# Tile 0's multi-query preparation moved into the last feed-forward block, and mixing weights applied to the queries

## The chip, the cores and the metric

One core of one Trainium2 chip runs the whole kernel in one launch. The metric is device time in microseconds. PE is TensorE, PEld its weight load, DVE is VectorE, ACT is ScalarE, POOL is GpSimd, SP is SyncE, which issues the DMAs.

## The reference

Input x is 16 sequences of 256 tokens with 128 channels, fp32. Four residual layers follow each other, each on a layer-normalised input:

```python
x = x + attn_a(layernorm(x))   # 32 heads of 4, two decaying scans (m = 0, 1), own layer norm
x = x + ffn(layernorm(x))      # sum over 8 experts of (silu(x Wg) * (x Wu)) Wd, FFN 512
x = x + attn_b(layernorm(x))   # 16 query heads of 8, one key and value head, causal softmax
x = x + ffn(layernorm(x))      # the same weights again

# attn_a, per token; phi(u) = elu(u) + 1, beta clipped, mix a softmax over m
S = S * beta[m] + phi(k) v
K = K * beta[m] + phi(k)
num, den = phi(q) . S, phi(q) . K + eps
y = sum over m of num / den * mix[m]
```

## The kernel before

A tile is 512 tokens, that is two sequences; there are 8. The program has three stages, and each engine's order of instructions is written out by hand. Engines meet at counting semaphores; PE, as every engine, takes its instructions strictly in order.

**Stage A.** A loop over t = -1 to 9 runs 32 chunks (c = 0 to 31) in each step. In step t, attention A works on tile t (`attn(t, c)` of each engine says what is done in which chunk), its output layer norm on tile t-1 (`old`), and the first feed-forward on tile f = t-2. So steps 0 and 1 have no feed-forward, steps 2 to 7 have both, step 8 has feed-forward and the last tile's layer norm, and step 9 has feed-forward alone. A feed-forward chunk (`ffn_pe`) is three products of three matmuls: gate and up of chunk c, and `down` of chunk c-3. ACT makes silu (L537) and the high half of the product (`hidden_hi`, L547); DVE multiplies gate by up (L577, "the multiply"); the low half (`hidden_lo`, L553) is made by DVE for even chunks and by POOL for odd ones. PE may write the up bank of chunk c only when the multiply of c-2 has been done. In step 2 the weights are also split into halves: `hi_part` on ACT (L461) and `lo_part` on POOL (L466), from the staging buffer WS with room for two experts, and stored to a split copy that later steps load.

In attention A, DVE runs ten scans over 512 positions (L1534): for each m four numerator components and one denominator (z). The products with phi(q) (PQ) follow: m = 0 on DVE (L1541), m = 1 on POOL (L743), five components each. PE adds heads with fp32 matmuls: `numerator` (L1107), 8 of 128x512, and `denominators` (L1117); DVE takes the reciprocal (L1609, L1611) and makes WGT (L1616); PE spreads WGT over the partitions for each m (`weights`, L1128), ACT copies it out (L927), DVE multiplies with the numerators (`weighted`, L1518), and POOL adds the two (L768) into Y, which `project_y` (L1135, L1139) projects in chunk 0 of the next step.

**Stage B.** `run_slots` goes over tiles -1 to 8, two slots of 12 steps (k) each. Tile t's slots make the score rows of tile t (`rows`, L1255), while `nxt` = t+1 is prepared: layer norm applied, transposed (L642), four projections (`project_b`), values (`project_v`), and five selection products (`query_stack`, `key_stack`), each with a hop to ACT or DVE and back. Tile -1 has no rows: its slots are the preparation of tile 0 alone. Before them stand three last `down` products, the copy and transpose back (L560, L529), the residual (L585), zero and pattern writes on ACT (L1052, L1056), the constants of stage B on POOL, and the bias columns (L1434).

**Stage C.** The second feed-forward for the 8 tiles, as in step 9.

Of the kernel before, what the change touches and what calls it, by code (L numbers as in the profile page):

```python
# [16 lines left out]
F32 = mybir.dt.float32  # L17
# [6 lines left out]
P = 128  # L24
# [18 lines left out]
OUT_STEP = 5  # L43
CH = NE * FC
# [87 lines left out]
def run_steps(eng, step):  # L132


    for n in (-1, 0, 1):
        step(Tile(n, n % 2))
# [7 lines left out]
def program(nc, a_x, a_Wq, a_Wk, a_Wv, a_Wbeta, a_bbeta, a_Wmix, a_bmix, a_Wout, a_bout, a_ln_g, a_ln_b,  # L144
            b_Wq, b_bq, b_Wk, b_bk, b_Wv, b_bv, b_Wo, b_bo, f_Wg, f_Wu, f_Wd, consts, out):
    ctx = ExitStack()
    with ctx:  # L147
# [82 lines left out]
        WS = take(2, 3, FFN)  # L230
# [22 lines left out]
        RS = take(MA, TOK)  # L253
# [33 lines left out]
        XH = take(TOK, dt=F32R)  # L287
        XL = take(TOK, dt=F32R)
        QST = take(2, NJ, TOK, dt=F32R)
        QKH = take(2, TOK, dt=F32R)  # L290
        QKL = take(2, TOK, dt=F32R)
        NMP = take(2, NJ, P, dt=F32R)
        KST = take(2, NG, TOK, dt=F32R)
        VS = take(2, SUB, 2 * P - RG, dt=F32R)
        Q2 = take(NJ, SEQ, dt=F32R)
        PH = take(RING, TOK, dt=F32R)
        PL = take(RING, TOK, dt=F32R)

# [5 lines left out]
        A = sems("a", "u_k u_q ex_k ex_q re_k re_q phi_k phi_q clip scaled beta scan prod0 prod1 num0 num1 den dp rc "  # L304
                      "wgt rep rs ay y z zsum zg zb done")
# [9 lines left out]
        F = sems("f", "wload0 wload1 store0 store1 sg su sd wh wl gate up sil mul hh hl hlp d ys back done")  # L315
# [26 lines left out]
        def is_tile(n):  # L342
            return 0 <= n < NT

# [102 lines left out]
        def load_part(sp, x, part):  # L447

            after(sp, F.wl, 3 * (x - 2) + part + 1)
            dst = WS[:, x % 2, part, :]  # L450
# [3 lines left out]
            sp.dma_start(dst, src).then_inc((F.wload0, F.wload1)[x % 2], 16)  # L454

        def hi_part(act, x, part):

            act.wait_ge((F.wload0, F.wload1)[x % 2], 48 * (x // 2 + 1))
            after(act, (F.gate, F.up, F.d)[part], FC * (x - 1))
            after(act, (F.store0, F.store1)[x % 2], 48 * (x // 2))  # L460
            act.activation(W2[:, x % 2, part, 0, :], WS[:, x % 2, part, :], ACT.Copy).then_inc(F.wh, 1)  # L461

        def lo_part(g, x, part):

            g.wait_ge(F.wh, 3 * x + part + 1)
            g.tensor_tensor(W2[:, x % 2, part, 1, :], WS[:, x % 2, part, :],  # L466
# [114 lines left out]
        def residual(v, f):  # L581
# [3 lines left out]
            v.tensor_tensor(xs, xs, by_sub(bank[6]), ALU.add).then_inc(F.done, 1)  # L585
# [70 lines left out]

        VAT = P - RG
# [1138 lines left out]
```

## Time and profile before

| | us |
|---|---|
| median of 3 runs | 1755.48 (1751.98 to 1756.20) |
| the profiled execution's own time | 1751.74 |
| its span, first to last instruction | 1749.9 |

PE is busy in 1625.6 us of the span (93%), DVE in 1071.4 (61%), ACT in 1014.7 (58%), POOL in 886.4 (51%). Matmuls overlap in the records (each lasts some 0.39 us and the next starts 0.23 us later), so a high busy share of PE does not by itself say that PE sets the pace. Step t of stage A with feed-forward can be told by the first multiply (L577) of each tile: steps 3 to 7 start at 212.6, 301.4, 390.2, 479.0 and 567.8 us, 88.8 us apart.

### The profile page before, as it was taken

How to read it: one execution, taken by the hardware profiler on the slowest of the kernel's cores; microseconds unless marked ns; L12 is line 12 of the kernel's file. 1: busy time of each engine (PE TensorE's matmuls, PEld its weight loads, DVE VectorE, ACT ScalarE, POOL GpSimd, SP SyncE). 2: the span in 40 equal slices, each digit the busy share in tenths (PEclk: the TensorE clock that was granted, in tenths of full speed). 3: DMA queues.
4: the chain of work that ended last, by engine and by line, in shares of the span. 5: the costliest groups of instructions: out<-in, count | busy, mean ns of one | idle time of the engine just before them, and what ended most of it. 6: DMA issues, size and time to landing. Idle time of an engine off the chain costs nothing. (4 is left out here: it accounts for less than half of the span.)

```text
span 1749.9 us, 24769 instructions
## 1 busy us (share of the span) xinstructions
PE 1625.6 (93%) x7232; PEld 1253.1 (72%) x7232; DVE 1071.4 (61%) x1871; ACT 1014.7 (58%) x1871; POOL 886.4 (51%) x793
## 2 busy tenths in 40 slices
PE   3588999999999999995899999997999999999998
PEld 2356777777777878883566666665888888888887
DVE  5667777777778685452676676652554555554544
ACT  2236474747464646552577787785555555555554
POOL 3668664646464544333477777784333332333332
PEclk9888999999999999995999999998999999999999
DMA  4035444444443435640000000002555556555553
GB/s 122 1 110 197 151 146 143 145 145 145 141 146 135 145 136 189 212 157 0 1 1 2 2 1 0 1 16 81 181 192 204 194 182 207 193 188 195 195 199 133
DMA packets 72548, 215.88 MB, mean 123 GB/s; under 512 B 7387, under 2 KB 20832, under 8 KB 72416
## 3 DMA queue, kind: packets, MB, share of 16 engines
q1 hardware_dynamic: 72416, 214.35, 35.7%
q8 instruction: 55, 0.90, 0.2%
q14 instruction: 77, 0.63, 0.1%
HBM read 199.64 MB, written 14.68 MB: 122 GB/s over the span
## 5 line engine op out<-in xcount | busy, mean ns | idle before, releaser
L553 POOL TENSOR_TENSOR ARENA_R<-ARENA,ARENA_R 128x512 fp32r<-128x512 f32 x256 | 344.3, 1345 | 605.6 <-ACT ARENA_R L547 604.9
L577 DVE TENSOR_TENSOR ARENA<-ARENA,pair 128x512 f32<-128x512 f32 x512 | 349.2, 682 | 453.7 <-PE pair L340 417.2
L537 ACT ACTIVATE ARENA<-bank 128x512 f32<-128x512 f32 x512 | 306.3, 598 | 471.5 <-PE bank L340 470.5
L338 PE MATMUL pair<-ARENA_R 128*128 128x512 f32 x1064 | 416.9, 392 | 18.6 <-POOL ARENA_R L553 8.3
L340 PE MATMUL pair<-ARENA_R 128*128 128x512 f32 x1064 | 415.0, 390 | 0.0
L339 PE MATMUL pair<-ARENA_R 128*128 128x512 f32 x1064 | 414.3, 389 | 0.0
L547 ACT ACTIVATE ARENA_R<-ARENA 128x512 fp32r<-128x512 f32 x512 | 319.6, 624 | 32.8 <-DVE ARENA L577 30.9
L871 POOL TENSOR_TENSOR ARENA_R<-ARENA,ARENA_R 128x512 fp32r<-128x512 f32 x192 | 249.4, 1314 | 79.9 <-ACT ARENA L1048 76.3
L338 PE MATMUL bank<-ARENA_R 128*128 128x512 f32 x568 | 239.7, 422 | 23.3 <-DVE ARENA L1524 18.1
L338 PEld LDWEIGHTS pair<-ARENA_R 128*128 128x128 f32 x1064 | 200.8, 189 | 67.9 <-POOL ARENA_R L553 10.0
L340 PEld LDWEIGHTS pair<-ARENA_R 128*128 128x128 f32 x1064 | 200.9, 189 | 42.3
L339 PEld LDWEIGHTS pair<-ARENA_R 128*128 128x128 f32 x1064 | 201.1, 189 | 41.2
L339 PE MATMUL bank<-ARENA_R 128*128 128x512 f32 x568 | 223.5, 393 | 0.0
L340 PE MATMUL bank<-ARENA_R 128*128 128x512 f32 x568 | 223.4, 393 | 0.0
L553 DVE TENSOR_TENSOR ARENA_R<-ARENA,ARENA_R 128x512 fp32r<-128x512 f32 x256 | 195.0, 762 | 0.1
L1648 DVE TENSOR_REDUCE ARENA<-bank 128x2 f32<-128x512 f32 (+1 forms) x192 | 131.0, 689 | 86.5 <-PE bank L1257 56.4
L338 PEld LDWEIGHTS bank<-ARENA_R 128*128 128x128 f32 x568 | 108.2, 190 | 52.4 <-DVE ARENA L1524 21.8
L1293 PE MATMUL pair<-ARENA_R 128*128 128x512 f32 x384 | 135.2, 433 | 8.5 <-ACT ARENA L1028 6.9
L1048 ACT ACTIVATE ARENA_R<-pair 128x512 fp32r<-128x512 f32 x192 | 115.6, 602 | 34.4 <-PE pair L1281 26.0
L339 PEld LDWEIGHTS bank<-ARENA_R 128*128 128x128 f32 x568 | 108.4, 191 | 23.5 <-issue 4.3
L340 PEld LDWEIGHTS bank<-ARENA_R 128*128 128x128 f32 x568 | 107.9, 190 | 23.3
L1534 DVE TENSOR_TENSOR_SCAN ARENA<-ARENA 128x512 f32<-128x512 f32 x80 | 121.5, 1526 | 0.0
(213 smaller groups left out, 2037.7 us busy)
## 6 DMA issues: line engine op xcount, KB each, us to landing
ARENA_R<-split_weights SPq DMA_DIRECT2D x360, 512.0 KB, 4.8
split_weights<-ARENA_R SPq DMA_DIRECT2D x24, 512.0 KB, 3.8
X<-in_L_attn_a_x_dram SPq DMA_DIRECT2D x8, 256.0 KB, 5.5
ARENA<-in_L_ffn_Wg_dram SPq DMA_DIRECT2D x8, 256.0 KB, 2.9
ARENA<-in_L_ffn_Wu_dram SPq DMA_DIRECT2D x8, 256.0 KB, 3.2
ARENA<-in_L_ffn_Wd_dram SPq DMA_DIRECT2D x8, 256.0 KB, 3.8
out_dram<-X SPq DMA_DIRECT2D x8, 256.0 KB, 4.3
CST<-in_tables_dram SPq DMA_DIRECT2D x1, 835.5 KB, 4.5
```

Of the source, the lines that this page charges most:

```text
L338: pe.matmul(dst, wh, xh, start=start, stop=False)
L339: pe.matmul(dst, wh, xl, start=False, stop=False)
L340: return pe.matmul(dst, wl, xh, start=False, stop=stop)
L537: act.activation(SG[:, c % 2, :], bank[c % 2], ACT.Silu).then_inc(F.sil, 1)
L547: act.activation(HH[:, G % FC, :], HF[:, G % FC, :], ACT.Copy).then_inc(F.hh, 1)
L553: eng.tensor_tensor(HL[:, G % FC, :], HF[:, G % FC, :], HH[:, G % FC, :].bitcast(F32), ALU.subtract).then_inc(lo_done(G)[0], 1)
L577: v.tensor_tensor(HF[:, c % FC, :], SG[:, c % 2, :], bank[2 + c % 2], ALU.mult).then_inc(F.mul, 1)
L871: g.tensor_tensor(PL[:, u % RING, :], PT[:, u % RING, :], PH[:, u % RING, :].bitcast(F32), ALU.subtract).then_inc(B.pl, 1)
L1048: act.activation(dst[:, u % RING, :], bank[2 + u % 2], ACT.Exp, scale=DB ** -0.5).then_inc(B.t_used, 1)
L1293: m = pe.matmul(bank[4 + qb], VS[:, p, 2 * ob + kb, at:at + P], (PH, PL)[i][:, u % RING, :], start=(u < 2 and i == 0), stop=(g == NG - 1 a ...
L1534: v.tensor_tensor_scan(S[:, m, c, :], BETA[:, m, :], KV[:, c, :], 0.0, ALU.mult, ALU.add).then_inc(A.scan, 1)
L1648: v.tensor_reduce(dst, src, AX.X, ALU.max, negate=True).then_inc(B.row_used, 1)
```

## The change

It has two parts.

Part 1: the slots of tile -1 are gone (`run_steps` starts at 0). Their work and the constants are done by `ramp(c)` on each engine, in chosen chunks of step 9 among the feed-forward chunks. The last `down`, the transpose back (now through bank 5) and the residual are put into the first slot of tile 0. The buffers are laid out anew so that tile 0's own (KST0, QST0, QKH, QKL, VS) overlap nothing of the feed-forward; for this WS has room for one expert and its next load waits for that expert's own split. SP moves its wait for attention A and nine small loads one expert earlier, and adds a wait for the last column scores (B.t_ready) before the second expert's load of stage C.

Part 2: denominators come first (both z scans, both products on POOL, `denominators` in chunk 15, reciprocal in 16, `weights` for both m in chunk 18). DVE then makes PQM[m] = PQ * weight[m], the numerator products use PQM, POOL adds the two scales in SBUF (`sum_scales`), and PE sums heads once, in 4 matmuls instead of 8, in chunks 27 and 30. ACT copies the bank to Y.

```diff
@@ run_steps @@
-    for n in (-1, 0, 1):
+    for n in (0, 1):
@@ SP @@
-                if n in (2, 3):
+                if n == 2:
                     for part in range(3):
-                        load_part(sp, n - 2, part)
+                        load_part(sp, 0, part)
...
+                if x == NE * NT + 1:
+                    sp.wait_ge(B.t_ready, UNITS * NSEQ)
@@ POOL, attention A @@
-                    if c in (19, 21, 22, 23, 24):
-                        product(t, (19, 21, 22, 23, 24).index(c))
-                    if c == 30:
-                        g.wait_ge(A.ay, 2 * (t + 1))
-                        after(g, A.z, t)
-                        g.tensor_tensor(Y[:, :], RS[:, 0, :], RS[:, 1, :], ALU.add).then_inc(A.y, 1)
+                    if c in (13, 14):
+                        product_z(t, c - 13)
+                    if c in (20, 24, 26, 27):
+                        product(t, (20, 24, 26, 27).index(c))
+                    if c in (23, 25, 27, 28):
+                        sum_scales(t, (23, 25, 27, 28).index(c))
@@ POOL, step 9 @@
+            def ramp(c):
+                if c == 1:
+                    b_rstd(g, T0)
+                if c == 3:
+                    prep_weights()
+                if c == 5:
+                    prep_bias_rows()
+                if c == 7:
+                    prep_splits()
+                if c == 9:
+                    prep_biases()
+                if c in (11, 13):
+                    prep_stacks(range(c - 11, c - 9))
+                if c == 14:
+                    rotated(T0, 0)
+                if c == 15:
+                    prep_keys()
+                if c == 17:
+                    prep_masks()
+                if c == 18:
+                    rotated(T0, 1)
+                if c == 26:
+                    b_rstd(g, T1)
@@ ACT, attention A @@
-                    if c == 27:
-                        weight_rows(t, 0)
-                    if c == 28:
-                        weight_rows(t, 1)
+                    if c == CH - 1:
+                        act.wait_ge(A.num, t + 1)
+                        after(act, A.z, t)
+                        act.activation(Y[:, :], bank[7], ACT.Copy).then_inc(A.y, 1)
@@ PE, attention A @@
+                if is_tile(t) and c == 15:
+                    pe.wait_ge(a_used["v2"], t + 1)
+                    denominators(t)
...
-                    if c == 20:
-                        pe.wait_ge(a_used["v3"], t + 1)
-                        numerator(t, 0, (0, 1))
-                    if c == 22:
-                        numerator(t, 0, (2, 3))
-                        pe.wait_ge(a_used["v2"], t + 1)
-                        denominators(t)
-                    if c == 24:
-                        pe.wait_ge(n_a.lo, min(t + 2, NT))
-                        after(pe, n_f.lo, t)
-                        numerator(t, 1, (0, 1))
-                    if c == 25:
-                        numerator(t, 1, (2, 3))
-                    if c == 26:
+                    if c == 18:
                         weights(t, 0)
+                        weights(t, 1)
                     if c == 27:
-                        weights(t, 1)
+                        pe.wait_ge(A.pq, 2 * (t + 1))
+                        numerator(t, (0, 1))
+                    if c == 30:
+                        numerator(t, (2, 3))
@@ PE, step 9 @@
+                if c == 8:
+                    pe.wait_ge(F.done, NT - 1)
+                    b_turn(pe, T0)
...
+                if c in (10, 12, 14, 16):
+                    pe.wait_ge(pr.wb, 10)
+                    project_b(T0, (c - 10) // 2)
+                if c == 18:
+                    pe.wait_ge(pr.wb, 15)
+                    project_v(T0, range(SUB))
+                if c == 20:
+                    pe.wait_ge(pr.selr, 2 * NJ + 3 + 3 + 1)
+                if 20 <= c < 20 + NJ:
+                    query_stack(T0, c - 20)
+                if c == 24:
+                    key_stack(T0)
@@ PE, first slot of tile 0 @@
+                    if opening(t, b, k, (0, 0)):
+                        down(pe, NT * CH - 1)
+                    if opening(t, b, k, (0, 2)):
+                        back(pe, NT - 1, bank[5])
@@ DVE, attention A, by chunk @@
+  11: key_value 0, scan(0, 4)   12: scan(1, 4)   13: key_value 1, 2   14: scan(0, 0)
+  15: key_value 3   16: reciprocal   17: WGT, scan(0, 1)   18: scan(1, 0)
+  19: weighted(0), weighted(1)   20, 21: scan(0, 2), scan(0, 3)   22: product(0, 2)
+  23: scan(1, 1)   24: product(2, 4)   25: scan(1, 2)   26: scan(1, 3)
```

The last hunk is written out by chunk from the diff of DVE's order. Before, the scans stand in chunks 12 to 23, the products of m = 0 in 17 and 19, the reciprocal in 24, WGT in 25 and `weighted` in 28 and 29.

## Rows read from the trace of the kernel before

**Rows 1.** Windows: start:end, us, then PE, PEld, DVE, ACT, POOL busy (instructions), granted clock, DMA share, GB/s.
```profile
112.10:212.70 100.60, 91.75 (x366) 69.83 (x366) 75.27 (x104) 58.95 (x110) 80.72 (x63) 0.94 0.53 185
390.20:479.00 88.80, 86.76 (x378) 68.48 (x378) 68.20 (x104) 49.86 (x91) 46.59 (x42) 1.00 0.41 142
724.00:789.60 65.60, 65.23 (x290) 53.70 (x290) 33.52 (x57) 38.14 (x69) 25.33 (x29) 1.00 0.48 165
790.40:832.28 41.88, 21.22 (x55) 12.71 (x55) 9.27 (x26) 11.80 (x16) 12.29 (x27) 0.54 0.00 0
832.28:848.40 16.12, 13.18 (x44) 7.32 (x44) 12.50 (x29) 1.23 (x2) 1.29 (x1) 0.82 0.00 0
```
**Rows 2.** Timeline of PE at stage A's end: start, us, line, [idle before <-releaser].
```profile
788.73 0.50 PE L338 MATMUL pair<-ARENA_R 128*128 128x512 f32 x1 [0.37 <-POOL ARENA_R L553]
789.99 0.40 PE L340 MATMUL pair<-ARENA_R 128*128 128x512 f32 x1
...
801.93 1.86 PE L1434 MATMUL bank<-ONES,ARENA 1*128 1x1 f32 x8 [0.78 <-DVE X L585]
...
832.28 0.79 PE L1255 MATMUL bank<-ARENA_R 128*128 128x512 f32 x1 [2.52 <-ACT ARENA_R L1011]
```
**Rows 3.** Timeline of DVE in step 5.
```profile
418.23 0.69 DVE L577 TENSOR_TENSOR ARENA<-ARENA,pair 128x512 f32<-128x512 f32 x1 [4.57 <-ACT ARENA L537]
...
448.08 1.21 DVE L1534 TENSOR_TENSOR_SCAN ARENA<-ARENA 128x512 f32<-128x512 f32 x1
...
449.80 1.40 DVE L553 TENSOR_TENSOR ARENA_R<-ARENA,ARENA_R 128x512 fp32r<-128x512 f32 x1
...
464.44 0.69 DVE L577 TENSOR_TENSOR ARENA<-ARENA,pair 128x512 f32<-128x512 f32 x1 [0.27 <-PE pair L340]
...
479.05 0.69 DVE L577 TENSOR_TENSOR ARENA<-ARENA,pair 128x512 f32<-128x512 f32 x1 [0.49 <-PE pair L340]
```
**Rows 4.** Timeline of PE in step 5.
```profile
449.77 1.88 PE L1107 MATMUL bank<-ARENA,CST 128*128 128x512 f32 x4
451.49 1.89 PE L1117 MATMUL pair<-ARENA,CST 128*128 128x256 f32 x8
```
**Rows 5.** Timeline of POOL in step 5.
```profile
428.59 0.61 POOL L368 TENSOR_TENSOR NB<-NM,RSTD 128x4 f32<-128x4 f32 x1
...
449.37 1.28 POOL L743 TENSOR_TENSOR ARENA<-ARENA 128x512 f32<-128x512 f32 x1 [2.89 <-DVE ARENA L1534]
```
**Rows 6.** Groups of DVE, 418.2 to 464.4: xcount | busy us, mean ns | idle before.
```profile
L1534 DVE TENSOR_TENSOR_SCAN ARENA<-ARENA 128x512 f32<-128x512 f32 x10 | 14.9, 1485 | 0.0
...
L553 DVE TENSOR_TENSOR ARENA_R<-ARENA,ARENA_R 128x512 fp32r<-128x512 f32 x9 | 8.3, 924 | 0.0
L1541 DVE TENSOR_TENSOR ARENA<-ARENA 128x1024 f32<-128x1024 f32 x2 | 4.6, 2310 | 0.0
```
**Rows 7.** Timeline of steps 0 and 1, each engine.
```profile
32.08 1.29 DVE L1511 SCALAR_TENSOR_TENSOR ARENA<-ARENA 128x512 f32<-128x512 f32 x2 [3.62 <-ACT ARENA L916]
...
44.13 1.20 DVE L1541 TENSOR_TENSOR ARENA<-ARENA 128x1024 f32<-128x1024 f32 x1
...
61.79 0.51 PE L1135 MATMUL bank<-BBA,ONESR 128*128 128x512 f32 x1 [2.75 <-POOL ARENA L768]
...
78.69 1.26 DVE L1511 SCALAR_TENSOR_TENSOR ARENA<-ARENA 128x512 f32<-128x512 f32 x2
...
84.90 0.80 POOL L368 TENSOR_TENSOR NB<-NM,RSTD 128x4 f32<-128x4 f32 x1
...
107.73 2.50 POOL L466 TENSOR_TENSOR ARENA_R<-ARENA,ARENA_R 128x512 fp32r<-128x512 f32 x2 [5.09 <-ACT ARENA_R L461]
...
109.14 0.77 PE L338 MATMUL bank<-ARENA_R 128*128 128x512 f32 x1 [2.65 <-POOL ARENA_R L466]
...
116.82 0.62 ACT L461 ACTIVATE ARENA_R<-ARENA 128x512 fp32r<-128x512 f32 x1
```
**Rows 8.** The page's DMA issues: KB each, us to landing.
```profile
ARENA<-in_L_ffn_Wd_dram SPq DMA_DIRECT2D x8, 256.0 KB, 3.8
```

More of the change, by code:

```diff
@@ L314, in program @@
                       "q2_ready q2_used t_ready t_used pl vhi pv os turn oc ro o ot otc out done")
-        F = sems("f", "wload0 wload1 store0 store1 sg su sd wh wl gate up sil mul hh hl hlp d ys back done")
+        F = sems("f", "rg ru rd store0 store1 sg su sd wh wl gate up sil mul hh hl hlp d ys back done")
         stored = sem("stored")
@@ L854, in _ @@
                     if t == NT + 1:
-                        prepare_b(c)
+                        ramp(c)
                     if (t, c) == (NT, 14):
-                        prepare_b(-1)
+                        g.wait_ge(A.done, NT)
+                        g.memset(BB[:, :], 0.0).then_inc(pr.ones, 1)
             hidden_lo(g, NT * CH - 1)
-            b_rstd(g, Tile(0, 0))
-            g.wait_ge(F.done, NT)
+            g.wait_ge(F.d, NT * CH)
             def slot(t, b):
@@ new lines, in _ @@
+            act.wait_ge(pr.bmix, 2)
+            for t in range(-1, NT + 2):
+                for c in range(CH):
+                    f = t - 2
+                    if is_tile(f):
+                        if is_tile(f - 1) and c == 3:
+                            take_down(act, f - 1)
+                        ffn_act(act, f, c)
+                    elif f == -1 and c >= CH - FC and part_at(f, c):
+                        hi_part(act, *part_at(f, c))
+                    attn(t, c)
+                    if t == NT + 1:
+                        ramp(c)
@@ L1238, in _ @@
                     attn(t, c)
-            for G in range(NT * CH - 3, NT * CH):
-                down(pe, G)
-            pe.wait_ge(F.done, NT - 1)
-            back(pe, NT - 1)
-            SQ, SL, SK, SKL, SID = 0, NJ, 2 * NJ, 2 * NJ + 1, 2 * NJ + 2
+                    if t == NT + 1:
+                        ramp(c)
+            down(pe, NT * CH - 3)
+            down(pe, NT * CH - 2)
             def rows(t, b, k):
@@ L1602, in attn @@
                     if c == 22:
+                        product(t, 0, 2)
+                    if c == 23:
+                        scan(t, 1, 1)
+                    if c == 24:
+                        product(t, 2, 4)
+                    if c == 25:
                         scan(t, 1, 2)
[L1604 removed]
+                    if c == 26:
                         scan(t, 1, 3)
[L1606 to L1611 removed]
@@ L1629, in _ @@
                     if t == NT + 1:
-                        if c == 12:
-                            v.wait_ge(F.done, 1)
-                            b_stats(v, Tile(0, 0))
-            b_apply(v, Tile(0, 0), range(SUB))
-            residual(v, NT - 1)
+                        ramp(c)
             def maximum(t, b, k):
```

449 lines of the change are left out of this document (248 added, 201 removed).

## Prediction

> **What bounds the kernel now.** I read the windows first, cut by step [rows 1]. Three kinds of stretch differ. Step 9, feed-forward alone, has 290 PE instructions in 65.6 us, one per 0.226 us, and PE busy throughout: PE sets that pace (9 matmuls, 2.04 us a chunk), while DVE is busy 33.5 us, ACT 38.1, POOL 25.3. The ramp from 790.4 to 832.28 us is the opposite: PE works 21.2 of 41.9 us at a granted clock of 0.54, about the lower of its two levels (1.2 and 2.4 GHz) after a stretch with little work, and no other engine is busy for even a third of the time. It is a chain of hops between engines. Steps 3 to 7, 88.8 us each, look PE-bound (86.8 busy). The timeline of DVE says otherwise for half of them: from the multiply of chunk 9 at 418.23 to that of chunk 26 at 464.44 DVE has no idle entry (the row at 464.44 is the first with one) [rows 3], 46.2 us in which PE is held at most two chunks ahead. So two limits alternate, DVE in the middle of a step, PE at both ends. The rest of stage B and stage C are touched only at the handover between them.
>
> **Part 1, the ramp.**
> Removed: PE's last `down` but one ends its issue at 789.99 + 0.23 = 790.22, rows of tile 0 begin at 832.28 [rows 2]: 42.1 us. The late POOL low half before it (PE idle 0.4 at 788.73 [rows 2], since POOL was making constants) goes too: 42.5.
>
> Paid in step 9, which is PE-bound, at 0.226 us a matmul [rows 1]: four projections 12 x 0.226 = 2.7; five selection products 10 x 0.226 = 2.3; four transposes, at 128 columns between 0.1 and 0.226 each, 0.4 to 0.9, I take 0.4; bias columns 1.86 us for eight at the low clock [rows 2], so 0.9 at the high one, 1.9 at most; values, 13 short matmuls, 0 to 2.9, I take 1.4. Together 7.7 (5.5 to 10.7).
>
> Cover for the rest: DVE's 9.3 us, ACT's 11.8 and POOL's 12.3 of the ramp [rows 1] go into step 9, where DVE has 32 us free, ACT 27 and POOL 40. Were the cover gone they would stand on the path again. Each hop has a chunk or more between issue and use: `project_b` i+1 stands two chunks behind i, so DVE's turn (multiply, low half, rope, three instructions of about 0.7) fits before PE returns after 2.7 us. A late hop stops PE, and behind it gate and up of the next chunk, for which ACT and DVE wait. For some 15 hops I take 1 us in all, 0 to 8. ACT's wait for `key_stack` in chunk 24 holds silu by about 0.5, inside the two chunks of slack.
>
> Moved into tile 0's first slot: last `down` 0.7 plus its wait for POOL's low half 0.4, transposes 0.4, residual 0.7 on DVE: 2.2. Today that slot lasts 16.1 us with DVE busy 12.5 at clock 0.82 [rows 1]; with the clock already up I give back 1.5. Net +0.7 (-1.5 to +2.5).
>
> SP: the nine small loads come one expert earlier, their wait (A.done) is over before; the wait for B.t_ready holds one expert's load, which is needed four chunks, 8 us, into stage C and lands in 4.8 [rows 8]: nothing. The single staging buffer: expert 1's first load is now issued after POOL's `lo_part` of about 109.0 and lands some 3.8 later [rows 7, 8], 112.8, while ACT uses it at 116.8 [rows 7]; later ones have four chunks. Nothing, at worst 4 us once.
>
> Part 1: -42.5 + 7.7 + 1 + 0.7 = -33; bounds -38 to -21.
>
> **Part 2, steps 3 to 7.** PE: an fp32 matmul of 512 columns costs (451.49 - 449.77)/2 = 0.86 us [rows 4]; four go, -3.44 a step. If PE bounded the whole step that would be the gain. But in DVE's 46.2 us: z product moved to POOL -0.7, scan (1, 3) moved behind the multiply of 26 -1.2, two `weighted` moved in +1.4: -0.5.
> DVE also pays for POOL. Against 1.21 for a free scan [rows 3], 0.69 for a low half (the same shape as a multiply) and 1.20 for a double product [rows 7], the groups show 1.485, 0.924 and 2.31 [rows 6]: 2.8 + 2.1 + 2.2 = 7.1 us, over POOL's 13 big operations of the stretch: 0.55 each. POOL's own count goes from 6 to 10 a step (two z, four products, four sums); inside the stretch 13 becomes 14: +0.6.
> The new wait: DVE's reciprocal in chunk 16 needs the denominators. POOL ends its statistics at 429.2 [rows 5], then z 1.28, a low half 1.3, z 1.28: 433.1; PE 1.7: 434.8. DVE would be there at about 434.6 and, with PE's chunk 16 behind the denominators, gets its multiply late: +1.2. Behind it on DVE are five scans; PE waits for them only through `down` and the multiply.
> So the multiply of 26 comes 1.3 later. From it to the next step's first multiply are 14.6 us now (464.44 to 479.05 [rows 3]), with two weights and a wait on ACT in them. Afterwards: six chunks 12.2, two numerator pairs 3.4, 1.5 of waits (0.9 for the multiply of 25, 0.6 for POOL's last sum), less 4.4 by which PE is ahead of the multiply of 26: 12.7, -1.9. Net -0.6 a step, -3 for five. Bounds: -3.4 a step (all PE) to +3.
> Rule and row on the coupling: the low half on DVE that starts at 449.80 while POOL works from 449.37 to 450.65 takes 1.40 and not 0.69 [rows 3, 5]. The Trainium skill, SBUF — State Buffer, section Who interferes with whom, says that a DVE instruction with two SBUF inputs and a GpSimd one that reads SBUF exclude each other for a whole instruction, the second waiting; the row agrees (it ends 0.55 after POOL). By that rule each added operation could cost DVE up to 1.28 and not 0.55, 0.9 instead of 0.6 in this stretch if all of it hits; a schedule in which more of them hit is the third rival.
>
> **Part 2, steps 0, 1 and 2.** No feed-forward fills steps 0 and 1, the chain itself counts. Step 0 takes 28.4 us from phi's end (32.08 + 1.29) to `project_y` at 61.79 [rows 7]. New, from phi's end: key times value and z scans 2.9, second z product to 4.4, denominators at the low clock to 6.3, reciprocal and WGT 8.9, two scans 11.2, `weighted` 12.5, two scans and the next tile's split 15.4, three scans and two double products with POOL alongside 24.7, then product, sum, sum 28.6, last numerator and Y copy 30.6: +2.2. Step 1 has the same, and its z products wait for POOL's statistics, which end at 85.7, 5.8 after phi's end (78.69 + 1.26) [rows 7], where step 0 needed them from 1.7: about +3 more. Both: +7.4 (+2 to +12). Behind POOL's sums stand `lo_part`s, for which PE's first gate (109.14 [rows 7]) waits.
> Step 2 (100.6 us) has POOL busy 80.7 [rows 1]. Four more operations, 1.28 to 2.2 each, 5 to 9 us, in stretches that are full; PE gives back 3.4. I take +4 (-2 to +8).
>
> **Sum.** -33 + 7.4 + 4 - 3 = -24.6 against the profiled execution's own 1751.7: 1727.1. That execution lies 3.7 below the median of the runs; from the median the sum gives 1730.9. Of the three runs two lie near the median and one near the profiled one; I take 1728, nearer to the sum's own execution.
>
> **Rivals.**
> 1. PE bounds all steps: five at -3.4, step 2 at -2, steps 0 and 1 at +5. 1755 - 33 - 17 - 2 + 5 = 1708. For: PE's 86.8 busy [rows 1]. Against: DVE without idle for 46 us [rows 3]. Chance 0.17.
> 2. POOL costs more in the steady steps, through late z products or sums: +2 each, steps 0 to 2 +14. 1755 - 33 + 10 + 14 = 1746. Chance 0.2.
> 3. The other side: POOL's four added operations a step land in full on DVE or the path, 4 x 1.28 = 5.1 in eight steps, 41 in all, and the chain of steps 0 and 1 costs 2 for its added hops: 1755 - 33 + 43 = 1765. It decides from (33 - 2)/8 = 3.9 us a step. Against: DVE is idle in the last five chunks, where three of the added operations stand. Chance 0.03. This is the schedule that the Trainium skill's rule above (SBUF — State Buffer, Who interferes with whom) allows at worst.
> 4. The preparation does not hide: 15 hops with a chunk of 2.04 us lost at most of them, 24 us in step 9. 1728 + 23 = 1751. Against: the hops' slack above. Chance 0.06, half of it within 0.3%.
> The forecast, 0.54.
>
> **Numbers.** Range 1708 to 1746: it reaches to rival 1 and rival 2 and leaves out under 0.2. A measurement of this kernel tells about 0.3%, 5.3 us, from no change. Faster: 0.54 + 0.17 + 0.2 + part of rival 4 = 0.94; same 0.03; slower 0.03.
>
> **What would show it.** Step 9: first multiply to last longer by about 8.5 us, PE without gaps over 0.5. PE from the last `down` but one to tile 0's rows: under 1 us, clock 1.00. Steps 3 to 7: 88.2 us each, DVE without idle in chunks 9 to 25 but for about 1 us before the reciprocal; if 85.4, rival 1. Step 1's end 7 us later than 109.1; step 2 near 104.6. I am wrong if the denominators hold PE in chunk 15 by more than 2 us, if PE waits for POOL's sums in chunk 30, or if a selection product waits for POOL's tables.

## The result, and the profile after

| | before | after |
|---|---|---|
| median of the runs, us | 1754.6 (1752.0 to 1756.2) | 1738.1 (1737.6 to 1739.2) |
| ratio, 95% interval | | 0.9908 [0.9891, 0.9925] |
| profiled execution: time, span, us | 1751.7, 1749.9 | 1739.2, 1737.4 |
| granted clock of TensorE over the span | 0.969 | 0.970 |

Faster, and inside the range of 1708 to 1746, but by 16.5 us of median and not by the 26.6 that lie between 1754.6 and the forecast 1728. The two profiled executions differ by only 12.5 us: the one before was faster than each of its four timed runs, and the one after is the slowest of its four.

The windows show the same kinds of stretch as [rows 1]: step 2, step 5, step 9, and the 12 us around the handover from stage A to stage B.
```profile
130.20:234.70 104.50, 87.61 (x355) 65.68 (x354) 73.57 (x102) 58.25 (x109) 84.97 (x66) 0.95 0.53 186
412.30:501.20 88.90, 84.60 (x371) 66.51 (x370) 70.30 (x104) 49.31 (x90) 53.88 (x46) 1.00 0.41 143
745.80:819.00 73.20, 73.20 (x335) 60.08 (x334) 45.83 (x81) 45.50 (x83) 38.48 (x57) 1.00 0.42 148
819.00:831.00 12.00, 10.30 (x45) 6.06 (x44) 9.21 (x16) 4.54 (x5) 1.70 (x2) 1.00 0.00 0
```
The low-clock ramp is gone: the handover stretch has clock 1.00 and PE busy 10.3 of 12 us. Step 9 has 335 PE instructions and PE is never idle in it. In step 5 PE is busy for 2.2 us less than before and the step lasts as long; POOL is busy for 7.3 us more, DVE for 2.1 more.

The timeline of PE at the handover (start, us; the last `down` but one is the group that ends with the row at 820.17) answers to [rows 2]:
```profile
820.17 0.39 PE L346 MATMUL pair<-ARENA_R 128*128 128x512 f32 x1
820.40 0.40 PE L1379 MATMUL bank<-ARENA_R 128*128 128x512 f32 x1
...
826.75 0.50 PE L344 MATMUL bank<-ARENA_R,WBH 128*128 128x512 f32 x1 [1.36 <-DVE ARENA_R L662]
```
Tile 0's rows (L1379) follow `down` at once; before, 42.1 us lay between.

Where the 12.5 us come from, by the start of the first feed-forward multiply of each step on DVE (L577 before, L587 after):

| stretch | before | after | difference | forecast |
|---|---|---|---|---|
| start to step 2 (steps 0 and 1) | 112.1 | 130.2 | +18.1 | +7.4 |
| step 2 | 100.6 | 104.5 | +3.9 | +4 |
| steps 3 to 7, five | 444.0 | 443.7 | -0.3 | -3 |
| step 8 | 67.4 | 67.4 | 0 | 0 |
| step 9 to the start of stage C | 491.7 | 457.5 | -34.3 | -33 |
| stage C and the end | 534.1 | 534.1 | 0 | 0 |

One line is far off: steps 0 and 1. These rows are from them, PE first, then DVE and POOL; they answer to [rows 7]:
```profile
39.30 3.75 PE L1191 MATMUL pair<-ARENA,CST 128*128 128x256 f32 x8 [2.98 <-POOL ARENA L759]
...
60.75 2.08 PE L1182 MATMUL bank<-ARENA,CST 128*128 128x512 f32 x2 [2.20 <-POOL ARENA L771]
65.33 3.78 PE L1182 MATMUL bank<-ARENA,CST 128*128 128x512 f32 x4 [2.50 <-POOL ARENA L771]
69.80 0.79 PE L1209 MATMUL bank<-BBA,ONESR 128*128 128x512 f32 x1 [0.69 <-ACT ARENA L996]
...
97.71 3.75 PE L1191 MATMUL pair<-ARENA,CST 128*128 128x256 f32 x8 [3.10 <-POOL ARENA L759]
```
```profile
55.23 2.22 DVE L1629 TENSOR_TENSOR ARENA<-ARENA 128x1024 f32<-128x1024 f32 x1
57.37 4.41 DVE L1623 TENSOR_TENSOR_SCAN ARENA<-ARENA 128x512 f32<-128x512 f32 x2
...
101.50 0.42 DVE L1679 TENSOR_SCALAR ARENA<-pair 128x256 f32<-128x256 f32 x1 [4.94 <-PE pair L1191]
```
```profile
54.25 2.11 POOL L771 TENSOR_TENSOR ARENA<-ARENA 128x512 f32<-128x512 f32 x1 [2.87 <-DVE ARENA L1629]
56.32 2.24 POOL L765 TENSOR_TENSOR ARENA<-ARENA 128x512 f32<-128x512 f32 x1
58.70 1.99 POOL L771 TENSOR_TENSOR ARENA<-ARENA 128x512 f32<-128x512 f32 x1
60.66 3.39 POOL L765 TENSOR_TENSOR ARENA<-ARENA 128x512 f32<-128x512 f32 x2
64.02 2.47 POOL L771 TENSOR_TENSOR ARENA<-ARENA 128x512 f32<-128x512 f32 x2
```
Three things are to be seen. The denominators (L1191) and the last numerators (L1182) take twice what [rows 4] show for them: 3.75 against 1.89. DVE's double product takes 2.22 where the free one takes 1.20, and two scans 4.41 where two free ones, 1.21 each by [rows 3], would take 2.4. And POOL works from 54.25 to 66.49 with hardly a break, each operation 2.0 to 2.2 while DVE runs, and the last numerator waits for it. In the windows of 10 us the granted clock is 0.54 from 50 to 60 us, where PE is busy for 2.0, and 0.50 from 60 to 70, the lower of its levels, 1.2 GHz.

One theory went into the runs, with rivals to it. Theory A: the parts are independent; POOL's four sums a tile, through the time that POOL and DVE take from each other, and PE at its lower clock level make steps 0 and 1 longer, and the sums eat in steps 3 to 7 what PE saves. The rivals are that the parts disturb each other (B), that DVE and POOL alone (C) or PE alone (D) set the pace of steps 3 to 7, that the extra hop between engines costs whatever its length (E), and that the clock is no cause (F). Rivals G to J, and Theory H, belong to the later kernels and are told in their expectations.

### The profile page after: what moved, and what is told of

Read it like the earlier page. It is cut to its first block and busy times, and to the rows that moved or that the text cites. A ratio compares the mean times of both kernels' runs of the same rounds, so it can differ in the third digit from the quotient of the medians.

```text
span 1737.4 us, 24680 instructions
## 1 busy us (share of the span) xinstructions
PE 1601.0 (92%) x7168; PEld 1236.3 (71%) x7168; DVE 1087.5 (63%) x1863; ACT 1009.3 (58%) x1864; POOL 939.0 (54%) x825
## 5 line engine op out<-in xcount | busy, mean ns | idle before, releaser
L587 DVE TENSOR_TENSOR ARENA<-ARENA,pair 128x512 f32<-128x512 f32 x512 | 348.4, 681 | 449.2 <-PE pair L346 400.6
L346 PEld LDWEIGHTS pair<-ARENA_R 128*128 128x128 f32 x1064 | 200.6, 189 | 42.1
L563 DVE TENSOR_TENSOR ARENA_R<-ARENA,ARENA_R 128x512 fp32r<-128x512 f32 x256 | 205.0, 801 | 0.6
L1623 DVE TENSOR_TENSOR_SCAN ARENA<-ARENA 128x512 f32<-128x512 f32 x80 | 138.7, 1741 | 0.0
```

The source lines that it names most:

```text
L346: return pe.matmul(dst, wl, xh, start=False, stop=stop)
L563: eng.tensor_tensor(HL[:, G % FC, :], HF[:, G % FC, :], HH[:, G % FC, :].bitcast(F32), ALU.subtract).then_inc(lo_done(G)[0], 1)
L587: v.tensor_tensor(HF[:, c % FC, :], SG[:, c % 2, :], bank[2 + c % 2], ALU.mult).then_inc(F.mul, 1)
L1623: v.tensor_tensor_scan(S[:, m, c, :], BETA[:, m, :], KV[:, c, :], 0.0, ALU.mult, ALU.add).then_inc(A.scan, 1)
```

## The experiments

All kernels together; "first" is the start of the first multiply of step 2 (what steps 0 and 1 took), the columns behind it are lengths in us, all four from the one profiled execution. Ratios are against the kernel before, run on the same chip.

| kernel | median, us | ratio, 95% | first | step 2 | step 5 | step 9 to C |
|---|---|---|---|---|---|---|
| before | 1753 to 1754.6 | 1 | 112.1 | 100.6 | 88.8 | 491.7 |
| after | 1738.1 | 0.9908 [0.9891, 0.9925] | 130.2 | 104.5 | 88.8 | 457.5 |
| e1 part 1 alone | 1719.3 | 0.981 [0.9794, 0.9826] | 114.4 | 100.1 | 88.8 | 457.3 |
| e2 part 2 alone | 1772.0 | 1.0108 [1.0091, 1.0125] | 130.3 | 104.1 | 88.9 | 491.6 |
| e3 sums on PE | 1728.2 | 0.9861 [0.9844, 0.9877] | 118.3 | 102.3 | 89.0 | 459.3 |
| e4 no sums | 1712.8 | 0.9771 [0.9755, 0.9788] | 121.4 | 101.1 | 86.3 | 456.9 |
| e5 sums of 8 columns | 1714.7 | 0.9773 [0.9748, 0.9798] | 122.1 | 100.3 | 85.6 | 460.9 |
| e6 clock fill | 1734.5 | 0.9888 [0.9872, 0.9905] | 125.8 | 104.2 | 88.9 | 457.4 |
| e7 part 1, clock fill | 1723.6 | 0.9821 [0.9803, 0.984] | 120.6 | 100.7 | 88.8 | 457.5 |
| e8 z products first | 1735.3 | 0.9903 [0.9881, 0.9925] | 128.2 | 99.6 | 88.9 | 456.9 |
| e9 8 columns and fill | 1709.3 | 0.9752 [0.9736, 0.9769] | 120.5 | 101.8 | 85.6 | 457.1 |
| e10 sums late | 1755.5 | 1.0018 [1.0008, 1.0028] | 130.8 | 107.6 | 92.2 | 457.0 |
| e11 hybrid | 1731.4 | 0.9873 [0.9854, 0.9893] | 117.5 | 99.2 | 92.1 | 457.3 |
| e12 hybrid 2 | 1724.2 | 0.9833 [0.9819, 0.9847] | 118.3 | 99.1 | 88.8 | 457.3 |

"First" of kernels with the same code in steps 0 and 1 differs by up to 2.1 us (after and e8), so single microseconds in that column aren't read. Two entries of the last column are long in a place that their edits don't touch: in the profiled executions of e3 and e5 the granted clock fell once more early in stage B (0.72 from 823 to 829 us in e3, 0.61 from 808 to 821 in e5, where the kernel after has 1.00 from 834 to 847), and stage B took 1.8 and 3.4 us longer than in the kernel after. Totals of e3 and e5 are compared with this in mind, and the steps go by their own columns.

**e1 and e2: the parts by themselves.** e1 is the kernel after with the old queries, weights, products and order of scans; e2 is the kernel before with the new ones.

> Part 1 alone, part 2 undone. Theory A (the two parts are independent; part 2 costs 18 us in steps 0 and 1 and 4 us in step 2, and gives nothing in steps 3 to 7): steps 0 to 8 last as in the kernel before, the stretch from step 9 to stage C is 34 us shorter, so about 1754.6 - 34 = 1720 us, 18 us under the changed kernel. Rival B (part 1's single staging buffer and its new memory layout cost part of the 18 us, since expert 1's loads come later): step 2 starts later than 212 us - 112 us after the start here too, and the time is 1725 to 1735 us.

> Part 2 alone, part 1 undone. Theory A (independent parts): steps 0 and 1 together 18 us longer than before, step 2 4 us longer, steps 3 to 7 as before, the rest as before: about 1754.6 + 22 = 1776 us. Rival B (part of the loss comes from part 1): steps 0 and 1 lose under 12 us and the time is under 1769 us.

Theory A on both. Part 1 alone gives 0.981, part 2 alone 1.0108; their product, 0.9916, lies inside the interval measured for both together, 0.9908 [0.9891, 0.9925]. Steps 0 and 1 lose all of their 18 us with part 2 alone, and "first" is 2.3 later with part 1 alone, about what repeats of one code differ by. Rival B's times (1725 us or more for e1, under 1769 for e2) did not come. Part 2 is a loss of 1.1%.

**e3: the scales added on PE.**
```diff
 def numerator(t, comps):
     for c in comps:
-        pe.wait_ge(A.sum, 4 * t + c + 1)
-        x = pe.matmul(bank[7], cst(f"sum_{c}"), S[:, 0, c, :], start=(c == 0), stop=(c == DA - 1))
+        for m in range(MA):
...
+            x = pe.matmul(bank[7], cst(f"sum_{c}"), S[:, m, c, :], start=(c + m == 0), stop=(c + m == DA))
-                    if c in (23, 25, 27, 28):
-                        sum_scales(t, (23, 25, 27, 28).index(c))
```


> The changed kernel, but PE adds the two scales: eight fp32 matmuls of 512 columns in the numerator and no sum on POOL. PE's count goes back up by 4 x 0.86 = 3.44 us a step, POOL's goes down by four operations of 1.3 to 2.2 us. Theory A (PE sets the pace in the last chunks of a step, and POOL's sums cost DVE about 0.5 us each by holding it): steps 3 to 7 come out 1 to 2.5 us longer each (3.44 less the waits for the sums and the coupling), steps 0 and 1 2 to 4 us shorter each because two sums of 2.2 us leave their chain and one matmul of 1.9 us at the low clock comes in: 1735 to 1746 us in all. Rival C (DVE and POOL alone set the pace of steps 3 to 7): they become 1 to 2 us shorter each, and the time is 1722 to 1729 us. Rival D (PE alone): 3.44 us longer in each of steps 3 to 7, 1750 us or more.

10 us faster than the kernel after. The total missed Theory A's range and is in Rival C's, but not by its mechanism: steps 3 to 7 rose by 0.2 and did not fall. Theory A's 1 to 2.5 and Rival D's 3.44 aren't there either. The gain is in steps 0 and 1, which gave back 11.9 us where Theory A had 4 to 8, and in step 2 (2.2).

**e4 and e5: sums left out, sums of 8 columns.** e4 drops the sums and keeps four matmuls on the first scale; e5 keeps all waits and cuts the operands.
```diff
@@ e5, sum_scales @@
-g.tensor_tensor(S[:, 0, c, :], S[:, 0, c, :], S[:, 1, c, :], ALU.add).then_inc(A.sum, 1)
+g.tensor_tensor(S[:, 0, c, 0:8], S[:, 0, c, 0:8], S[:, 1, c, 0:8], ALU.add).then_inc(A.sum, 1)
```


> The changed kernel with POOL's four sums of each tile left out: the numerator adds the heads of the first scale only, so the second scale is missing from the attention output. PE's count is that of the changed kernel. Theory A (the sums cost steps 0 and 1 their own length on the chain, and steps 3 to 7 their coupling with DVE and the last wait): steps 0 and 1 4 to 6 us shorter each, step 2 2 to 4 us, steps 3 to 7 1 to 2 us each: 1738 - 10 - 3 - 7 = 1718 us. Rival D (PE alone sets the pace of steps 3 to 7, so the sums there cost nothing): steps 3 to 7 stay at 88.8 us, and the time is about 1726 us.

> The changed kernel with POOL's four sums of each tile cut from 512 columns to 8: the semaphores and the order stay, the duration goes (the second scale is missing in the other 504 columns). Theory A (what costs is the time that the sums hold POOL and the SBUF port beside DVE): like the kernel without sums, 1713 us within 3, steps 3 to 7 at 86.3 to 86.8 us. Rival E (the extra hop, DVE to POOL to PE, costs, whatever its length): near 1730 to 1738 us, steps 3 to 7 at 88 or more.

Steps 0 and 1 gave back 8.9 and 8.1 us, step 2 3.4 and 4.2, each of steps 3 to 7 2.5 and 3.2. The hop with its short operation costs nothing that shows, and the duration is what costs: Rival E is out, Rival D too. Theory A had steps 3 to 7 1 to 2 us shorter for e4 and at 86.3 to 86.8 for e5, so it priced the sums too low.

Step 5 of e5 (first line) and of e3 (second), in windows:
```profile
393.57:479.18 85.61, 83.17 (x370) 67.01 (x369) 66.13 (x104) 49.24 (x90) 51.90 (x46) 1.00 0.43 148
```
```profile
398.61:487.62 89.01, 86.57 (x378) 68.50 (x377) 67.27 (x103) 49.28 (x90) 48.46 (x42) 1.00 0.42 143
```
In both PE is idle for 2.44 us, and they differ by eight PE instructions, 3.40 us of PE: both are bound by PE, with the same small waits. e4, with e3's POOL and e5's PE instructions, is idle for 2.80. The kernel before had 88.80 - 86.76 = 2.04 idle in its step [rows 1]: by the same reading it was bound by PE as well, though no run takes work from PE alone in that kernel. In the kernel after PE is idle 88.90 - 84.60 = 4.3. So PE's saving of 3.4 is real, and the sums take 88.8 - 85.6 = 3.2 of it by e5, 2.5 by e4. Nearly all of that lies between the multiplies of chunks 9 and 26, where two of the four sums stand: this stretch lasts 47.65 us after, 45.55 in e4 and 44.52 in e5, and the rest of the step 13.2, 12.7 and 13.1.

e3 and e4 also bear on the clock. They have the same instructions on POOL and DVE, and e3 has four more numerator matmuls a tile, yet its "first" comes 3.0 us earlier. PE's last numerators of step 0 and the projection of Y, in e3 and then in e4:
```profile
54.16 9.87 PE L1184 MATMUL bank<-ARENA,CST 128*128 128x512 f32 x16 [5.86 <-DVE ARENA L1632]
65.05 1.05 PE L1216 MATMUL bank<-WOUT,ARENA 128*128 128x128 f32 x8
```
```profile
60.76 3.75 PE L1181 MATMUL bank<-ARENA,CST 128*128 128x512 f32 x4 [1.21 <-POOL ARENA L765]
65.79 1.91 PE L1212 MATMUL bank<-WOUT,ARENA 128*128 128x128 f32 x8
```
e3 works without a wait, its granted clock from 30 to 70 us is 0.74 where e4's is 0.66, and the projection takes 1.05 us and not 1.91. From the denominators of step 0 to those of step 1 it is 51.8 us in e3 and 54.3 in e4.

How they take it stands in the timelines of DVE and POOL in step 5, in chunks 22 to 24. The kernel after:
```profile
476.35 1.21 DVE L1629 TENSOR_TENSOR ARENA<-ARENA 128x1024 f32<-128x1024 f32 x1
477.49 0.67 DVE L587 TENSOR_TENSOR ARENA<-ARENA,pair 128x512 f32<-128x512 f32 x1
478.09 1.40 DVE L563 TENSOR_TENSOR ARENA_R<-ARENA,ARENA_R 128x512 fp32r<-128x512 f32 x1
479.41 2.31 DVE L1623 TENSOR_TENSOR_SCAN ARENA<-ARENA 128x512 f32<-128x512 f32 x1
481.64 0.65 DVE L587 TENSOR_TENSOR ARENA<-ARENA,pair 128x512 f32<-128x512 f32 x1
482.22 1.94 DVE L1629 TENSOR_TENSOR ARENA<-ARENA 128x1024 f32<-128x1024 f32 x1
```
```profile
477.64 1.29 POOL L771 TENSOR_TENSOR ARENA<-ARENA 128x512 f32<-128x512 f32 x1 [1.30 <-DVE ARENA L1629]
478.90 1.73 POOL L563 TENSOR_TENSOR ARENA_R<-ARENA,ARENA_R 128x512 fp32r<-128x512 f32 x1
481.80 1.28 POOL L765 TENSOR_TENSOR ARENA<-ARENA 128x512 f32<-128x512 f32 x1 [1.16 <-DVE ARENA L1623]
```
And e5, the same instructions of DVE, and POOL's short sum:
```profile
457.62 1.21 DVE L1629 TENSOR_TENSOR ARENA<-ARENA 128x1024 f32<-128x1024 f32 x1
458.75 0.67 DVE L587 TENSOR_TENSOR ARENA<-ARENA,pair 128x512 f32<-128x512 f32 x1
459.35 0.68 DVE L563 TENSOR_TENSOR ARENA_R<-ARENA,ARENA_R 128x512 fp32r<-128x512 f32 x1
459.95 1.21 DVE L1623 TENSOR_TENSOR_SCAN ARENA<-ARENA 128x512 f32<-128x512 f32 x1
461.08 0.66 DVE L587 TENSOR_TENSOR ARENA<-ARENA,pair 128x512 f32<-128x512 f32 x1
461.66 1.66 DVE L1629 TENSOR_TENSOR ARENA<-ARENA 128x1024 f32<-128x1024 f32 x1
```
```profile
458.91 0.20 POOL L771 TENSOR_TENSOR ARENA<-ARENA 128x8 f32<-128x8 f32 x1 [1.30 <-DVE ARENA L1629]
```
Read the first pair together: the sum runs from 477.64 to 478.93, DVE's low half of 478.09 ends only at 479.49, 0.56 after it (1.40 for an instruction of 0.68); POOL's next operation, a low half, is held in turn (1.73), and ends at 480.63, and the scan of 479.41 then ends at 481.72 (2.31 for 1.21). One sum has cost 0.7 + 1.1 = 1.8 us on DVE. From the double product's start to the next one's are 5.87 us here and 4.04 in e5. Behind it, at 482.35, PE has a wait of 1.16 us for the multiply of 481.64. In e5 POOL's low half of this place comes later, at 460.17, when ACT is done, and DVE's low half and scan run free. So e5 takes away the sum and also shifts what stands behind it; without any sum, in e4, the scans of the stretch are not all free either (below).

**e6, e7 and e9: extra matmuls to hold the clock.** Some 100 matmuls of constants in each of steps 0 and 1, into a free bank; e6 in the kernel after, e7 in part 1 alone, e9 with the short sums.
```diff
+FILL = {1: 4, 11: 10, 14: 10, 16: 4, 17: 4, 19: 4, 20: 4, ..., 30: 4, 31: 6}
+def filler(n):
+    for i in range(n):
+        pe.matmul(r3(bank[1], 4), LAH[:, i % 4, :], LAH[:, 0:4, :], start=True, stop=True)
+                if t in (0, 1) and (c - 1) in FILL:
+                    filler(FILL[c - 1])
@@ numerator, e6 and e9 only @@
+                    if t in (0, 1) and c % 2:
+                        filler(8)
```


> The changed kernel with some 100 extra matmuls of constants in each of steps 0 and 1, in places where PE waits, into a bank that nobody reads until step 2: they keep the clock up and compute nothing. Theory A (part of the 18 us of steps 0 and 1 is PE at its lower level: denominators 3.75 instead of 1.89 us, the last numerator pair 3.78 instead of 1.72, in both steps, and the weights and projections between): steps 0 and 1 together 6 to 10 us shorter, 1728 to 1732 us. Rival F (chain length and coupling alone, and the filler stands in the way of late hops): 1738 us or more.

> Part 1 alone with the same extra matmuls in steps 0 and 1. There the clock is low only in part of step 1 (0.50 from 80 to 90 us). Theory A: 2 to 4 us shorter than part 1 alone, 1716 us. Rival F: no shorter than part 1 alone, 1719 us or more.

> The changed kernel with the sums cut to 8 columns and with the extra matmuls of constants in steps 0 and 1, both at once (the second scale is missing in 504 columns). Of the 18.1 us that steps 0 and 1 lost, the short sums gave back 8.1 and the clock fill 4.4. Theory A (the two add up): the first multiply of step 2 comes at 117.7 us within 1.5, and 3.4 us are left for the longer chain itself (z products on POOL, late numerator); 1710 us. Rival F (the same time counted twice: the sums cost mainly by letting the clock fall): the first multiply stays at 120 us or later.

The window 30 to 70 us of the kernel after, then of e6:
```profile
30.00:70.00 40.00, 17.87 (x39) 8.94 (x38) 26.71 (x24) 5.00 (x10) 21.16 (x17) 0.63 0.00 0
```
```profile
30.00:70.00 40.00, 32.76 (x138) 24.27 (x137) 26.79 (x24) 5.49 (x11) 21.79 (x17) 1.00 0.00 1
```
The denominators in the timeline of PE of e6:
```profile
39.80 1.97 PE L1200 MATMUL pair<-ARENA,CST 128*128 128x256 f32 x8 [1.40 <-POOL ARENA L759]
```
The clock rises from 0.63 to 1.00 and the denominators (L1200 there) fall from 3.75 to 1.97. "First" comes 4.4 us earlier, less than the 6 to 10 expected, and the median is 3.6 us lower, with intervals of the ratios that overlap. e7 is a miss: the filler costs 6.3 us in steps 0 and 1, where PE had less idle time to fill. There PE is busy for 10.00 us of the window 50 to 60 and 9.98 of 60 to 70, so the filler stands in the way of what follows on PE. (The profiled execution is e7's slowest; the medians of e7 and e1 are 4.3 us apart, and the intervals of their ratios overlap.) e9 misses too: "first" comes at 120.5, Rival F's 120 or later; sums and fill together give 9.7 of the 18.1 us, against 8.1 and 4.4 alone. That favours Rival F's double counting, but the filler's own price, seen in e7, spoils the subtraction. The clock is a cause: e6 is 4.4 us earlier and e3 3.0 earlier than e4, both by more than the 2.1 of repeats. How much it costs in all is not settled.

**e8: z products first.** In POOL's loop the z products of chunks 13 and 14 stand ahead of the feed-forward low halves of the same chunk.
```diff
                     f = t - 2
+                    if is_tile(t) and c in (13, 14):
+                        product_z(t, c - 13)
                     if is_tile(f):
                         ffn_pool(g, f, c)
```


> The changed kernel with POOL's two z products ahead of the feed-forward low halves of chunks 13 and 14. Theory A (in step 2 PE waits 4.9 us for the second z product, which stands behind two weight low halves and one hidden one, and comes back at the low clock): the stop of PE ahead of the denominators falls under 1.5 us, step 2 is 4 to 6 us shorter (98.5 to 100.5 us), steps 3 to 7 are 0 to 1 us shorter each; 1729 to 1734 us. Rival G (the low halves that now come later stop PE instead): step 2 stays above 103 us and the time at 1738 us.

Theory A for step 2: 99.6 us, 4.9 less. PE's row of its denominators in e8:
```profile
174.60 1.97 PE L1191 MATMUL pair<-ARENA,CST 128*128 128x256 f32 x8 [0.92 <-POOL ARENA L759]
```
In the kernel after the same row has a wait of 4.89 us and takes 3.75:
```profile
179.69 3.75 PE L1191 MATMUL pair<-ARENA,CST 128*128 128x256 f32 x8 [4.89 <-POOL ARENA L759]
```
Steps 3 to 6 did not move, and step 7 got 2.3 us longer (90.7 against 88.3), where Theory A had each of them up to 1 us shorter: between its chunks 13 and 16 the second z product runs beside a low half on DVE, which takes 1.40 us and not 0.68, and the granted clock of the step is 0.98 where it was 1.00. The median, 1735.3, lies above the forecast 1729 to 1734 and is not told apart from that of the kernel after.

**e10, e11 and e12: attempts at a better kernel.** e10 moves the sums to chunks 27 to 30 and the numerators to 29 and 31. e11 does so from tile 3 on, adds on PE in tiles 0 to 2, and has the z products first. e12 is e11 with the sums in pairs, and another order of DVE in steps 0 and 1. The diff shows e12 against e11.
```diff
@@ e12, POOL @@
-                    if t >= 3 and c in (27, 28, 29, 30):
-                        sum_scales(t, c - 27)
+                    if t >= 3 and c in (27, 29):
+                        sum_scales(t, c - 27)
+                        sum_scales(t, c - 26)
@@ e12, DVE @@
+                    if c == 16 and t < 2:
+                        scan(t, 0, 1)
+                        if t == 1:
+                            scan(t, 1, 0)
                     if c == 16:
                         v.wait_ge(A.den, t + 1)
...
```


> The changed kernel with POOL's four sums moved behind all its products, to chunks 27 to 30, where DVE is idle, and the two numerator pairs to chunks 29 and 31. Theory H (a sum costs only where it holds a DVE instruction of the stretch without idle, chunks 22 to 26, and what was called POOL's hold on DVE is that): the multiply of chunk 26 comes 2 to 3 us earlier, steps 3 to 7 last 86.0 to 87.5 us; steps 0 and 1 lose 2 us each, since four sums now stand in a row at the end of their chain; about 1732 us. Rival I (PE then waits at the end of the step for the last sum and for the copy of Y): steps 3 to 7 at 88.5 us or more, 1740 us or more.

> The changed kernel with three edits: in tiles 0 to 2 PE adds both scales (eight matmuls, no sum on POOL), from tile 3 on POOL's sums stand in chunks 27 to 30 with the numerators in 29 and 31, and the z products stand ahead of the feed-forward low halves. It computes the whole reference. Theory A with H: steps 0 and 1 as with all sums on PE (first multiply of step 2 at 118 us), step 2 at 97 to 99 us, steps 3 to 7 at 86.0 to 87.5 us: 1709 to 1718 us, under part 1 alone (1719). Rival I: 1722 us or more.

> The hybrid with two more edits, each read from its own steps; it computes the whole reference. (1) In tiles 0 and 1 DVE runs one scan (tile 0) or two (tile 1) ahead of the reciprocal, in the 2.3 and 4.9 us in which it stood idle for the denominators. Theory A (that idle time is what is left of steps 0 and 1 once the sums are gone): Y of step 1 comes 3 to 5 us earlier than with the sums on PE, the first multiply of step 2 at 113 to 115 us. Rival J (the wait only moves to the weights, since denominators, reciprocal and weights are the chain): 117 us or more. (2) From tile 3 on the sums stand in pairs in chunks 27 and 29, ahead of the feed-forward low half of chunk 29 and not behind it. Theory H (the 90 to 92 us of the late sums came from the last sum behind that low half, which waited for PE through ACT, while PE's numerator waited for the sum): steps 3 to 7 at 86 to 87.5 us. Rival I (sums this late hold PE whatever their order): 88.8 us or more. With both, 1706 to 1714 us; with neither, 1728 or more.

In steps 0 to 2 e11 came close to what Theory A said (117.5 for 118, and 99.2 for 97 to 99). Theory H fell. Its first half held: the stretch from the multiply of chunk 9 to that of chunk 26 shrank from 47.65 to 45.6 us in all three. But from there to the next step's first multiply it grew from 13.2 to 18.5 us in step 5 of e10 and e11. PE and then POOL of e11:
```profile
478.58 1.10 PE L1191 MATMUL bank<-ARENA,CST 128*128 128x512 f32 x2 [0.28 <-POOL ARENA L771]
481.38 1.76 PE L1191 MATMUL bank<-ARENA,CST 128*128 128x512 f32 x2 [1.70 <-POOL ARENA L771]
```
```profile
479.62 2.93 POOL L771 TENSOR_TENSOR ARENA<-ARENA 128x512 f32<-128x512 f32 x2
485.65 1.29 POOL L563 TENSOR_TENSOR ARENA_R<-ARENA,ARENA_R 128x512 fp32r<-128x512 f32 x1 [3.10 <-ACT ARENA_R L557]
486.90 1.29 POOL L771 TENSOR_TENSOR ARENA<-ARENA 128x512 f32<-128x512 f32 x1
```
The last sum (486.90) stands behind a feed-forward low half that waits 3.10 us for ACT; ACT waits for PE's gate, and the gate stands behind the numerator, which waited 1.70 for a sum. Part of the loss is the clock again: steps 3 and 4 of e10 and step 3 of e11 last 90.4 to 90.6 us at a granted clock of 1.00, the ones after them up to step 6 92.1 to 92.2 at 0.98. e12's pairs undo that ring: steps 3 to 6 last 88.8 us, with 15.2 us behind the multiply of 26, and step 7 lasts 90.6, as in e8. That is still no gain on the kernel after; what was won in the middle (2.1) is lost at the end (2.0). For the sums, Rival I's figures came out in all three kernels.

For steps 0 and 1 of e12 Rival J held: DVE's wait ahead of its reciprocal in step 1 fell from 4.94 in the kernel after to 1.51, 1.93 and 1.02 appeared ahead of the two `weighted`, and Y of step 1 is projected at 117.31 us, as in e3. e12's median, 1724.2, is under the 1728 said for neither edit helping and far above the 1714. Denominators, reciprocal and weights are the chain there, not DVE's order.

No kernel that computes the reference beat e1, part 1 alone: 1719.3 us.

## Why the prediction was right, and where it was off

The time came out 10.1 us above the forecast and 7.9 under Rival 2's 1746. The direction rests on part 1, which was right in size and in cause. Part 2 was forecast as a loss of 8.4 us (7.4 + 4 - 3) and cost 21.7: a loss as said, but two and a half times the size, and steps 0 and 1 alone went past their own bound. That the total still lies in the range is owed to its width of 38 us and not to the working of part 2. Rival 2's "late z products or sums" were real in steps 0 to 2 (22 us where it had 14), and absent as a net loss in steps 3 to 7 (-0.3 where it had 10).

- **Part 1, -33.** Measured -34.3: the 42.1 us between `down` and tile 0's rows are gone, step 9 up to there lasts 74.6 us and not 66.2 (+8.4; the forecast's 7.7 + 1), and from tile 0's rows to stage C it is 382.9 us where it was 383.5 (-0.6), against the +0.7 given. The ring of hops hid. Shown by e1.
- **Steps 0 and 1, +7.4.** Measured +18.1, above the bound of 12: the term that was mis-sized, and most of the miss of the sum (10.7 of 12.1 us). The forecast's "product, sum, sum 28.6" priced POOL's last operations as if the schedule left them free; with the sums on PE the loss is 6.3 us, with sums of 8 columns 10.0. And "denominators at the low clock 1.9" was a misreading: 1.89 in [rows 4] is the price at full clock, in a stretch at 1.00 by [rows 1]; at the lower level they take 3.75. PE waits more in the new chain, and the clock falls from 0.84 to 0.63 in comparable stretches (30 to 62 us before, 30 to 70 after). The 6.3 us that stay with the sums on PE are near the forecast's own longer chain, though at another mix of clock and hops.
- **Step 2, +4.** Measured +3.9. POOL's fullness was rightly the cause, but the place was not named: the second z product, behind the low halves, stops PE for 4.9 us, and e8 takes all of the loss away by putting it ahead. Leaving the sums out takes 3.4 of the 3.9 away as well (e4), so the two causes overlap, and that the balance of "5 to 9" against 3.4 gave the right figure is in part luck.
- **Steps 3 to 7, -0.6 each.** Measured -0.06. The two halves were near: the multiply of chunk 26 came 1.4 later (1.3 said), the rest of the step 1.4 shorter (1.9 said). But "two limits alternate, DVE in the middle of a step, PE at both ends" does not fit the kernel before. There, in the 46.2 us in which DVE had no idle entry [rows 3], PE was busy for 44.48, and it had two idle microseconds in the whole step; e3, e4 and e5 last as long as PE's work plus 2.4 to 2.8 us. Rival 1's view fits the kernel before, and its forecast of the kernel after was wrong, because the sums then did make DVE late. The four sums cost 2.5 us (e4) to 3.2 (e5), against the 0.6 that the forecast gave to POOL's added work beside DVE and 0.6 to the wait for its last sum; of the 3.2, 3.1 fall in the stretch with two of the sums, some 1.6 each.
- **The coupling.** The mean of 0.55 us for each POOL operation was an average over hits and misses. The scans of [rows 6] went from 1485 to 1742 ns in the mean and with the sums at 8 columns are back at 1498; but with no sums at all (e4) they stay at 1621, so the mean hangs on how POOL's other operations fall against DVE's as well. One sum was seen to cost 1.8. By the rule that the forecast cites, the one added operation of the stretch could cost 1.28 where it had 0.55; the 0.9 given there does not follow. The Trainium skill, SBUF — State Buffer, section Who interferes with whom, has the shared ports as an exclusive lock, held for a whole instruction. The rows at 478.09 and 479.41 agree: they end 0.56 and 1.09 us after the POOL operation that was ahead of each, within some 0.1 us of their free lengths, 0.68 and 1.21.
- **The total.** Against the profiled execution the sum was 1727.1 and the time 1739.2, 12.1 more; the median is 10.1 above the 1728 taken.
- **The signs of being wrong.** Two of the three came true, in steps 0 to 2 alone: denominators held PE by 2.98, 3.10 and 4.89 us, and in steps 0 and 1 PE waited 2.50 and 2.51 us for POOL's last sums. In step 5 the timeline of PE shows neither. Nothing stopped PE at a selection product in step 9.
- **Small slips without weight.** The terms of part 1's 7.7 add up to 6.3 at the least and not 5.5, and the 4.8 us ascribed to [rows 8] is the page's figure for the split weights, 512 KB; its row there for 256 KB says 3.8.

What stays open: how the 18 us divide between the clock and the hold of POOL and DVE on each other, which feed each other; and whether an order of POOL exists in which the sums cost nothing. The most that it could give is known from e5: 3.2 us in each of five steps.

## What to carry to other kernels

An engine without idle entries in a stretch need not be the limit of the period: compare the period with each engine's busy time, and look for the one whose busy time plus about the same idle time (2.0 to 2.8 us here, for PE) gives the period in variants too. Work moved from PE to GpSimd is not free because GpSimd has room: one add of 1.29 us was seen to cost DVE 0.7 us itself, and 1.1 more through the low half that it delayed on GpSimd. Where a chain leaves PE idle, ask at what clock PE comes back: here the denominators behind such waits took 3.75 us, and 1.97 at full clock. A chain of hops should be hidden behind bound work before it is shortened; that was all of the gain here, and it should have been shipped alone.

## What the runs showed of the hardware

- DVE's multiplies with one operand in PSUM were not held: 17 of them in the stretch of chunks 9 to 25 take 666 ns in the mean after and 663 before, while the scans beside them, with two SBUF operands, went from 1485 to 1742. The row at 481.64 (0.65 us) lies across the start of a POOL product at 481.80, and neither waits. The Trainium skill, SBUF — State Buffer, section Who interferes with whom, says the same of a DVE instruction with at most one SBUF input.
- A POOL add of 8 columns took 0.20 us where nothing held it (e5), one of 512 columns 1.29 (after).
- PE held at work by matmuls that nobody needs had a granted clock of 1.00 where it had 0.63 (e6), and the denominators 1.97 us where they had 3.75; the same filler where PE was needed came with a "first" 6.3 us later (e7).
- The same wait of PE was followed by either clock level: in e10 PE waits 1.70 us for a sum in steps 3 and 5 alike, and the numerator matmul behind it takes 1.13 us in step 3 (granted clock of the step 1.00, length 90.5 us) and 1.63 in step 5 (0.98, 92.2 us).
